# A graph network's neighbour sums read one run of 128 edges at a multiple of 32, from ring copies skewed by 32, 64 and 96 rows

## What is computed

```python
def _mean_agg(h, src, dst, deg):                       # L0: three SAGE layers (64 -> 128 -> 128 -> 64)
    summed = jax.ops.segment_sum(h[src], dst, num_segments=N_NODES)
    return summed / deg[:, None]
msg = norm[:, None] * xw[s]                            # L1: two GCN layers
out = jax.ops.segment_sum(msg, d, num_segments=num_nodes)
agg = jax.ops.segment_sum(x[src], dst, num_segments=N_NODES)   # L2: GIN
messages = _mlp(msg_in, mW1, mb1, mW2, mb2)            # L3: an MLP over each edge's two nodes and its 32 features
aggregated = jax.ops.segment_sum(messages, col, num_segments=nodes.shape[0])
x = _layernorm(x + _L3_gnn_ref(x, src, dst, edge_attr_32, ...), axis=-1)
```

## Time and profile before

| | |
|---|---|
| median of three runs | 5683.69 us |
| the profiled execution | 5690.94 us, its span 5689.2 us |
| PE, PE weight loads busy | 4874.8 us (86%), 4426.2 us (78%) |
| DVE, ACT, POOL busy | 3531.4 us (62%), 2906.9 us (51%), 3627.8 us (64%) |
| mean granted TensorE clock | 0.955 |
| sums, L690 | 22400 matmul records, 2702.4 us busy |
| moved by DMA | 812.14 MB, 143 GB/s |

### The profile page before, as it was taken

How to read it: one execution, slowest core, us unless ns; L and a number is a source line. 1 busy time by engine, 2 the same in 40 slices (tenths; PEclk the granted TensorE clock), 3 DMA queues, 4 the chain that set the end, 5 groups by cost and what they waited for, 6 DMA issues and landing times. The chain is left out here.

```text
span 5689.2 us, 127379 instructions
## 1 busy us (share of the span) xinstructions
PE 4874.8 (86%) x37818; PEld 4426.2 (78%) x37819; DVE 3531.4 (62%) x6596; ACT 2906.9 (51%) x7204; POOL 3627.8 (64%) x3226
## 2 busy tenths in 40 slices
PE   3999999969999799979996676659997799999998
PEld 2888888859999698969996666658886577777776
DVE  4454544547777488853334888847777356655555
ACT  0555555522222488854443888867775244344443
POOL 3544444337877577747776887757663777777772
PEclk9999999989999899989998888879999899999999
DMA  1444444435565577855554444435444222222222
GB/s 32 152 164 166 151 164 166 157 130 201 203 204 201 169 262 261 263 167 176 177 172 119 144 137 142 142 109 154 153 152 118 54 71 73 67 72 71 69 71 55
DMA packets 287987, 812.14 MB, mean 143 GB/s; under 512 B 89636, under 2 KB 90820, under 8 KB 265446
## 3 DMA queue, kind: packets, MB, share of 16 engines
q1 hardware_dynamic: 184998, 691.40, 34.0%
q0 software_dynamic: 102848, 119.09, 11.0%
HBM read 467.70 MB, written 340.81 MB: 142 GB/s over the span
## 5 line engine op out<-in xcount | busy, mean ns | idle before, releaser
L690 PE MATMUL ps_all<-arena 128*128 x22400 | 2702.4, 280 | 425.2 <-DMA arena<-y_t,ix_now 257.9
L690 PEld LDWEIGHTS ps_all<-arena 128*128 128x128 f32 x22400 | 2670.7, 198 | 488.4 <-issue 486.4
L636 POOL DMA_INDIRECT arena<-n_t,ix_now x800 | 932.4, 1166 | 413.9 <-issue 248.2
L636 POOL DMA_INDIRECT arena<-y_t,ix_now x800 | 904.5, 1131 | 349.8 <-issue 253.5
L657 DVE TENSOR_TENSOR arena<-iota,window 128x2048 f32<-128x2048 f32 x402 | 914.3, 2287 | 180.8 <-ACT bytes L1573 174.6
L636 POOL DMA_INDIRECT arena<-x_rows,ix_now x400 | 471.0, 1178 | 553.3 <-PE ps_all L690 436.7
L986 ACT ACTIVATE arena<-bytes 128x2048 f32<-128x2048 uint8 x300 | 562.0, 1903 | 150.6 <-DMA bytes<-hot_d 135.2
L1956 POOL DMA_INDIRECT store_a<-x_t,ix_now x400 | 437.5, 1094 | 219.2 <-issue 120.8
L1956 POOL DMA_INDIRECT store_a<-x_t,ix_dst x400 | 463.2, 1158 | 136.0 <-issue 135.4
L636 POOL DMA_INDIRECT arena<-x_t,ix_now x400 | 404.2, 1011 | 224.8 <-issue 120.8
L1463 PEld LDWEIGHTS ps_all<-w,tp 128*128 128x128 f32 x4000 | 478.9, 192 | 74.0 <-issue 73.2
(11 more groups left out here) (186 smaller groups left out, 7553.8 us busy)
## 6 DMA issues: line engine op xcount, KB each, us to landing
bytes<-hot_d SPq DMA_DIRECT2D x150, 512.0 KB, 7.4
x_t<-store_a SPq DMA_DIRECT2D x150, 512.0 KB
load_b<-x_t SPq DMA_DIRECT2D x150, 512.0 KB
s_t<-store_a SPq DMA_DIRECT2D x50, 1024.0 KB
n_t<-store_b SPq DMA_DIRECT2D x50, 1024.0 KB
load_a<-s_t SPq DMA_DIRECT2D x50, 1024.0 KB
y_t<-store_b SPq DMA_DIRECT2D x100, 512.0 KB
load_a<-x_cols SPq DMA_DIRECT2D x50, 512.0 KB
```

The source lines that it names most:

```text
L636: pool.indirect_dma_start(out=slot_rows(at, W, pitch), out_offset=None, in_=table, in_offset=bass.IndirectOffsetOnAxis(ap=ix_now[:, at:at ...
L690: last = pe.matmul(out(j, 2) if wide else out(j, 1), hot_matrices(at, j // GT)[:, k, j % GT, :], both(rows) if wide else rows, start=(k == ...
```

## The change

A node tile's edges are now taken to lie in one run of 128 edges that begins at a multiple of 32 (at the last such multiple before its first edge). So that such a run is one operand of a matmul, `arena` holds four rings of 64 slots instead of one: ring 0 as gathered, and rings 1 to 3, in whose slot s partition p holds the row of edge tile s if p is at least 32, 64 or 96, and of edge tile s+1 if it is less. The rows stay in their partitions; the one-hot matrix is made from a `window` that is put together in the same way (its third table, from `upper` and `apart`). The copies are DMAs from SBUF to SBUF, issued by SP: `skewed`, nine for an edge block, 786,432 bytes together. They wait for the gathered rows (in Update for the messages) and for the first half of the sums of two blocks before; PE's `rows_in` waits for the nine copies in place of the rows.

Sage1 keeps the two matmuls and the plain ring (`two_windows`). In the six other passes a tile's sum is one matmul, and one-hot matrices have half the size: 1024 columns for each of L657's instructions (now L684), L986's and L1573's, and 256 KB for a block in `hot_d`. In setup there are more small steps, a third table of places, and five DVE steps and three transposes for each of 7 chunks of `window`, where there were one and two. `dis` shares `deg`'s memory.

```diff
+SKEWS = 4
+STEP = P // SKEWS
-    window = sb("window", [P, 2, z.wide])
+    window = sb("window", [P, 3, z.wide])
-    dis = sb("dis", [P, z.tiles])
+    dis = deg
-    HOT = 2 * 2 * GT * P
-    RING_D, RING_H = RING * (D + 1), RING * H
+    HOT = NT * P
+    RING_D, RING_H = SKEWS * RING * (D + 1), RING * H
...
                     ve.wait_ge(S(f"wing{c % 2}"), 32 * (c // 2 + 1))
...
-                    V.tensor_scalar(win_f[:, c % 2, :, :], win_g[:, c % 2, :, :], tid[:, c:c + 1], None,
-                                    ALU.add).then_inc(S("winf"), 1)
+                    step(V.tensor_scalar(win_f[:, c % 2, 0:2, :], win_g[:, c % 2, :, :], tid[:, c:c + 1], None, ALU.add))
+                    step(V.tensor_scalar(upper, iota[:, :], skew_f[:, c:c + 1], None, ALU.is_ge))
+                    step(V.tensor_tensor(apart, win_f[:, c % 2, 0, :], win_f[:, c % 2, 1, :], ALU.subtract))
+                    step(V.tensor_tensor(apart, apart, upper, ALU.mult))
+                    step(V.tensor_tensor(win_f[:, c % 2, 2, :], apart, win_f[:, c % 2, 1, :], ALU.add))
+                    ve.sem_inc(S("winf"), 1)
...
         for j in tiles:
-            for k in range(2):
-                rows = ring[:, bass.ds(places[k][j - first] * W, W)]
+            for k in range(n):
+                rows = arena[:, bass.ds(places[k][j - first] * W, W)]
                 wide = W == D and j % GT < GT - 1
...
+            if windows:
+                for m in range(2):
+                    self.skewed(sp, m, m // 2, m % 2)
             for m in range(self.inputs_ahead):
                 next_inputs(m, m % 2)
             if windows and self.from_kept:
                 self.load_kept_last(sp)
+            if windows:
+                for m in range(2, self.skew_lead):
+                    self.skewed(sp, m, m // 2, m % 2)
 
             def body(m, i, u, v):
                 if windows:
+                    to = (u + self.skew_lead) % 2
+                    self.skewed(sp, m + self.skew_lead, i + (u + self.skew_lead - to) // 2, to)
                     self.sync_rows(sp, m, i, u, v)
...
+        two_windows = False
+        skew_lead = 2
+        SKEW_DMAS = 3 * (SKEWS - 1)
+
         def rows_in(self, pe, i, u):
-            pe.wait_ge(S(f"rows{u}"), landed(f"rows{u}", i, ET))
+            pe.wait_ge(S(f"skew{u}"), landed(f"skew{u}", i, self.SKEW_DMAS))
...
+        def skewed(self, sp, m, i, u):
...
+            self.rows_landed(sp, m, i, u)
+            sp.sem_inc(S("copying"), 1)
+            if not isinstance(m, int) or m >= 2:
+                sp.wait_ge(S("agg0"), before(m - 1))
+            sp.sem_inc(S("copying"), 1)
+            W, at = self.pitch, (m % RB) * ET
+            last = (at + (RING - 1)) % RING
...
+            for k in range(1, SKEWS):
+                low = k * STEP
+                for a, b, to, source, n in ((low, P, at, at, ET), (0, low, at, at + 1, ET - 1), (0, low, last, at, 1)):
+                    sp.dma_start(arena[a:b, ring_of(k, to, n)], arena[a:b, ring_of(0, source, n)]).then_inc(S(f"skew{u}"), 16)
```

More of the change, by code:

```diff
@@ L230, in setup @@
         tid = tb("tid", [P, z.wide // P])
-        win_g = tb("win_g", [P, 2, 2, P], I32)
-        win_f = tb("win_f", [P, 2, 2, P])
-        iota_i = tb("iota_i", [P, P], I32)
+        skew = tb("skew", [P, z.wide // P], I32)
+        skew_f = tb("skew_f", [P, z.wide // P])
+        win_g = part(4 * P).rearrange("p (c k e) -> p c k e", c=2, k=2)
+        win_f = part(6 * P, F32).rearrange("p (c k e) -> p c k e", c=2, k=3)
+        upper, apart = part(P, F32), part(P, F32)
+        iota_i = part(P)
         tid_i = tb("tid_i", [P, z.wide // P], I32)
@@ L449, in _ @@
                         pe.wait_ge(S("wins"), c - 1)
-                    for k in range(2):
+                    for k in range(3):
                         last = pe.transpose(ps[4 + c % 2][:, k * P:(k + 1) * P], win_f[:, c % 2, k, :], ident[:, :])
@@ L662, in kept_matrices, with places_of @@
     def kept_matrices(u, q):
-        return bytes8[u][:, :].rearrange("p (q k j n) -> p q k j n", q=2, k=2, j=GT)[:, q]
+        return bytes8[u][:, :].rearrange("p (q j n) -> p q j n", q=2, j=GT)[:, q]
     def kept_block(m):
         return hot_d[bass.ds(m * P, P), :]
-    def places_of(m, tiles):
+    def places_of(m, tiles, pairs=False):
         return [nc.values_load_multi_w_load_instructions(
-            slots[0:1, k, bass.ds(m * NT + tiles[0], len(tiles))], engines=(mybir.EngineType.PE,), min_val=0, max_val=RING - 1,
-            skip_runtime_bounds_check_because="the table holds remainders by RING")[1] for k in range(2)]
+            slots[0:1, k, bass.ds(m * NT + tiles[0], len(tiles))], engines=(mybir.EngineType.PE,), min_val=0,
+            max_val=(RING if pairs else SKEWS * RING) - 1,
+            skip_runtime_bounds_check_because="the table holds remainders by RING, and which of the skewed rings")[1]
+            for k in ((0, 1) if pairs else (2,))]
@@ L677, in sums @@
     def sums(pe, tiles, out, W, at, places):
-        first = tiles[0]
+        first, n = tiles[0], len(places)
         def both(ap):
@@ L686, in sums @@
         for j in tiles:
-            for k in range(2):
-                rows = ring[:, bass.ds(places[k][j - first] * W, W)]
+            for k in range(n):
+                rows = arena[:, bass.ds(places[k][j - first] * W, W)]
                 wide = W == D and j % GT < GT - 1
-                last = pe.matmul(out(j, 2) if wide else out(j, 1), hot_matrices(at, j // GT)[:, k, j % GT, :],
-                                 both(rows) if wide else rows, start=(k == 0), stop=(k == 1))
+                hot = hot_matrices(at, j // GT, True)[:, k, j % GT, :] if n == 2 else hot_matrices(at, j // GT)[:, j % GT, :]
+                last = pe.matmul(out(j, 2) if wide else out(j, 1), hot,
+                                 both(rows) if wide else rows, start=(k == 0), stop=(k == n - 1))
         return last
@@ L1105, in build @@
         tensor_behind = 4
+        skew_lead = 4
         from_kept = True
@@ L1471, in places @@
         def places(self, m, c):
-            return places_of(m, range(c * CT, c * CT + CT)) if exists(m) else None
+            return places_of(m, range(c * CT, c * CT + CT), self.two_windows) if exists(m) else None
         def collect_chunk(self, pe, m, i, u, c, places):
@@ L1506, in build, with rows_landed @@
         consumed = ("hid3",)
+        def rows_landed(self, sp, m, i, u):
+            if isinstance(m, int) and m == 0:
+                sp.wait_ge(S("zeros"), before(3))
+            super().rows_landed(sp, m, i, u)
         def load_block(self, sp, m, u):
@@ L1677, in build, with rows_in @@
         double = False
+        two_windows = True
+        def rows_in(self, pe, i, u):
+            pe.wait_ge(S(f"rows{u}"), landed(f"rows{u}", i, ET))
         loads = ((s1_t, load_a, H),)
```

92 lines of the change are left out of this document (60 added, 32 removed).

## The result

The changed kernel takes 5492.44 us (median; 5488.0 to 5500.35) beside 5683.64 us: 0.9668 of the time, 95% interval 0.9656 to 0.9679. In a second set it took 5503.89 beside 5678.55 us, 0.9686 (0.9666 to 0.9705); the kernel before, run once more as a kernel of its own in that set, 5674.35 us, 0.9995 (0.9985 to 1.0005). In the first set 191 us are gone, where 389 were predicted, and 5492 lies above the range, which ended at 5450. In two of the later sets the kernel before took 6222 and 6345 us, with hundreds of SP's small instructions (registers, semaphores) lasting 0.7 us, so ratios are compared within a set, and block times of those two are set only beside one another.

The account below looks back on a forecast made before the run. POOL was taken to bound every pass, or nearly, except Sage0, which was PE's. Terms -182 +15 +5 -65 -47 -115 +10 -10 sum to -389, from 5690.9 to 5302; the median 7 lower, 5295 us, range 5225 to 5450.

Parts of the forecast that it names:

- SP has the time: SP's queue: the copies fit in it, with five more DMAs a body in Sage2 taking 7 us of 11.
- they move 5 us back: SP's order: index load, next inputs, one-hot bytes and stores behind the copies come 5 us later.
- Sums, Sage0: Sage0: 32 of 64 PE records a block go, 3.8 us, giving 17.4 us a block: -182 us.
- Sage2: Sage2: no gain from sums, DMA load and late index loads give 11.36 us a block: +15 us (0 to +67).
- Gcn1: Gcn1: POOL's floor stays and DMA load reaches 9.2 of 10.48 us at worst: +5 us.
- Gcn2: Gcn2: halved one-hot instructions hold up gathers less, 0.4 us each instead of 1.25; 11.6 us a block: -65 us.
- Gin: Gin: POOL's wait for PE goes, with DVE nearly as close; 10.9 us a block: -47 us.
- Update: Update: less PE work, POOL waits and one-hot stalls give 21.7 us a block: -115 us.
- Clock: PE's clock falls in Sage2, Gcn1 and Gin as in Gcn2 (0.83), with work still below POOL: cost nothing.
- Setup, ends: Setup: small DMAs, a longer chain per chunk and small steps, +10 us; ends of Gin and Update together, -10 us.
- The closed loop: Rival: copies landing one behind another take 28 us and close the loop through POOL in four passes; 6002 us, chance 0.04.
- The rule on the port: Gathers beside one-hots: read as exempting L657, with two SBUF inputs, from holding up gathers; the prediction followed the row instead.

Follow-up runs that it names:

- six placed: Changed kernel with six copies a block instead of nine, their place in SP's body chosen by pass: 5235.98 us, 0.9216 of the kernel before.
- nine placed: Changed kernel with its nine copies a block, only their place in SP's body chosen by pass: 5277.48 us, 0.9302 of the kernel before.
- six copies: Changed kernel with SP's loop unrolled by eight blocks and six copies a block instead of nine: 5299.34 us, 0.9325 of the kernel before.

## Why the prediction was wrong, point by point

Lengths are from the first gather of a pass to that of the next, before and after; their sum is the difference of the spans, 203 us (Sage1 has -4). The prediction's number for it was 389. Sage2, Gcn2, Gin and Update miss their terms by 49, 48, 53 and 56 us, 206 together, and Sage0's luck of 23 us in the other direction hides a part. Two steps of the prediction failed, both on SP's queue: 'SP has the time', where SP came to be occupied for 11.8 of 12.4 us a block in Sage2, and 'they move 5 us back' of the loads behind the copies, priced at nothing where it cost Gcn2, Gin and Update about 1 us a block each.

- **What bounds the kernel before.** Right: Sage0 PE's, the others POOL's to about 0.3 us, with Gin and Update a little above. Six placed copies have Sage2, Gcn1 and Gin at 11.09, 10.44 and 10.50 us, which is POOL's pace.
- **Sums, Sage0** (-182): -205. The block is 17.10, not 17.4: PE's idle time shrank to 22.05 us in 23.5 blocks, 0.9 us a block, where I had kept 1.4.
- **Sage2** (+15): +64, just inside its upper bound of +67, but by another cause. The DMA engines were not it. The share of 0.89 times 12.4 us is 11.0 us a block, 9.0 before less 0.7 for the halved bytes, so the copies cost 2.7 us, inside 2.2 to 4.1; and six placed copies run at a share of 0.99 and 11.09 us. The failing step is 'SP has the time'. I had taken five more DMAs and 7 us of 11. SP was occupied for 3.5 us before, and 8.3 more now. A late index list, priced at 0 to 3 us every fourth block, cost 5 to 8; without it ('nine placed') Sage2 is at 11.53, SP's own pace.
- **Gcn1** (+5): -3. Right. Its head shows the latency of the copies: last gather, SP's copies, PE's first sum

```profile
2390.74 0.94 POOL L656 DMA_INDIRECT arena<-y_t,ix_now  x1 [0.30 <-issue]
...
2395.81 8.23 SPq L984 DMA_DIRECT2D arena<-arena  x10
...
2403.68 2.71 PE L721 MATMUL ps_all<-arena 128*128 x11 [30.47 <-DMA arena<-arena]
```

  12.9 us from the last gather's start to PE, 4.0 before: the copies take 8.9, forecast 8, and the loop through POOL held, as forecast.
- **Gcn2** (-65): -17. The stall was right: the stretch's gathers are busy 1.03 us on the mean (259.65/253), so that each of the two one-hot instructions costs POOL 0.33 us, forecast 0.4. Single gathers begun inside L686 last 0.94 to 1.96 us; one of them:

```profile
3310.87 1.22 DVE L686 TENSOR_TENSOR arena<-iota,window 128x1024 f32<-128x1024 f32 x1
3311.77 1.14 POOL L656 DMA_INDIRECT arena<-y_t,ix_now  x1 [0.30 <-issue]
```

  The step that failed is 'they move 5 us back', which I noted of the index load, the inputs and the stores and then priced at nothing. It is 6.6 to 7 us, and it lies in the loop from a block's output to the next inputs. With six copies Gcn2 is at 11.45, forecast 11.6.
- **Gin** (-47): +6. The same loop; 10.50 with six placed, forecast 10.9.
- **Update** (-115): -59. The same, by the edge features, for which PE waits 2 us a block; 21.64 placed, forecast 21.7.
- **Copies' price on SP**: nine at 0.52 us are 4.7 us. I had read the duration of one DMA instruction. The group of nine lasts 6.6 us in Gcn2, 0.73 us (median) from one to the next, since register instructions for the addresses stand between, and 7.9 us on the mean in Sage2.
- **Clock**: 0.83, 0.88, 0.71 and 0.86 in Sage2, Gcn1, Gcn2 and Gin, as forecast below 1.00, and it cost nothing that can be seen: Gcn2 has 0.71 at 12.58 us and 0.72 at 11.33 us.
- **Setup, ends** (0 together): +15 for setup. The ends of Gcn2 and Sage2 (last gather to the next pass's first) got 20 and 10 us longer, which I put down to the same late loads without a run that shows it, Update's and Sage0's 8 and 15 shorter.
- **The rivals.** The closed loop was the right kind of mechanism at the wrong place: it closed through SP and the input buffers, not through POOL and the ring. None of the rivals had SP as the bound. 'SP's nine issues took over 1 us each' stood among what would prove me wrong, and it did not happen: they are 0.7 to 0.9 us apart, and that was enough.
- **The rule on the port**, which the prediction set against the row, was misread; the last section has it.

With six placed copies, every pass is within 0.4 us a block of the forecast, each a little below it, and the span is 452 us below the kernel before, 63 more than forecast: what was missing from the sum was one engine's queue.

## What to carry to other kernels

When a change adds DMAs, add up the issuing queue as an engine of its own: the distance from one issue to the next, address instructions included, times their number, beside the queue's waits in the trace. Then walk the queue in order: what stands behind the new issues moves back by their whole length, and what wait stands ahead of them holds them up; put each group of issues behind waits that are already over and ahead of waits that are long. In this kernel moving one group of nine by a few statements was worth 226 us; by one statement in the wrong direction it cost 11 us a block in Update, in a set with slow SP instructions.

## What the runs showed of the hardware

- A gather of POOL that starts during one of DVE's one-hot instructions ends 0.8 us after that instruction does: L681 from 1401.84 to 1404.12, the gather until 1404.95; and in the earlier trace rows, the second of the pair until 3308.08, the gather until 3308.91. All 62 gathers begun inside L681 in 1150 to 1550 us of that run end 0.81 to 0.89 us after it; in Gcn2 seven that began in the first 0.04 us of an instruction were not held up (two before, five after the change). So the stall is what is left of the instruction when the gather begins, and shorter instructions cost less each: mostly 1.2 to 1.8 us for 2.28, 0 to 0.8 us for 1.22. The Trainium skill's page "SBUF — State Buffer" (SBUF: two separate sides) has a DVE instruction with two SBUF inputs block a GpSimd instruction only if the latter reads SBUF. L657 and L681 have two such inputs, and a gather takes its row numbers from `ix_now`, which lies in SBUF, so the rows agree with that rule if this counts as reading; the prediction took it for the exempt case. No run has a gather without such a list.
- A DMA share of 0.99 (six placed, Sage2) or 1.02 (nine placed) left the pass at 11.1 and 11.5 us, below the 12.3 us that the pass took at a share of 0.89: a share near 1 is no proof that the DMA engines are the bound.
- Copies from SBUF to SBUF of 786 KB a block took 2.7 us of all engines, by the shares of Sage2 above. By the Trainium skill's page "DMA: Bandwidth & Descriptors" (Where 436 GB/s comes from) an estimate is 1.8 us; the trace has half as much again.
